# Cross-attention of a two-block transformer on one core: key/value chunks of 384 keys, projection units issued in halves and in alternation, the last batch's values projected last

## The chip, the cores and the metric

The kernel runs on one core of a Trainium2 chip. The metric is device time in microseconds (us) of one execution; the time before is the median of three runs.

## What is computed

The reference sends x (8 sequences of 64 tokens, 512 features) through a small cross-attention, self-attention, an FP4-rounded feed-forward layer, a second cross-attention, an RWKV time mix, a channel mix and a small KAN layer. The change touches the second cross-attention alone: 16 heads of 32 features, 64 queries per batch against the 1601 context tokens of that batch, with learned relative-position terms.

```python
q = query @ Wq + bq; k = key @ Wk + bk; v = value @ Wv + bv     # key = value = ctx (8, 1601, 512)
attn1 = einsum('bhqd,bhkd->bhqk', rq, rk)
attn2 = einsum('bhqd,qkd->bhqk', rq, rel_k_table[rel_idx])
attn = softmax((attn1 + attn2) / sqrt(32))
x = attn @ rv + einsum('bhqk,qkd->bhqd', attn, rel_v_table[rel_idx])
return x @ Wo + bo
```

## The kernel before

`cross_attention` is written engine by engine; each engine runs its own instruction stream in program order and meets the others at semaphores. The order of the work is one hand-made list per **period** (`period`, L858), and every engine walks the same list and picks its own part of each item. Period p projects keys and values of batch p and, beside that, turns and weighs batch p-1, so there are nine periods for eight batches; the ninth only attends.

**Chunks.** The context comes in six chunks per batch, one of 321 keys (`FIRST_CH`) and five of 256 (`CH`, L812). SyncE loads a chunk into one of two `ctx_raw` buffers (`load_ctx`, L968) as soon as the chunk before last has been split. GpSimd splits it (L1058, L1061) into a rounded part `ctx_hi` and a rest `ctx_lo`, each with two buffers of its own, once TensorE has projected the chunk before last.

**Items.** `u` is a projection unit of twelve matmuls (`unit`, L1073): a key unit makes 128 features by the keys of a chunk (moving width 322 or 256), a value unit makes 128 keys by 512 features. Within a chunk come four key units, then two or three value units. Units write PSUM banks 4 and 5 in turn, so a unit waits for the copy of the unit two before it; ScalarE copies keys (VectorE those of the first chunk), VectorE copies values. `s` is a score job (`scores`, L1118): queries by the keys of a chunk into banks 0 to 3, for eight heads of the first chunk or all sixteen of another, copied to `E` with a running maximum by VectorE (L1349). After the last of the seven jobs VectorE makes `peak` and ScalarE runs `exponentials` (L1245), eight instructions over all 1601 keys. `t` is a turn (`turn`, L1138): four transposes of `E` into bank 6, copied by ScalarE to `ET` (L1243); the next turn waits for that copy. `p` (`weigh`, L1161) multiplies `ET` by the values. `r` (`inverse`, L1179) spreads the inverse sums with sixteen matmuls from `diag`, which VectorE makes in `diagonals` (L1356); ScalarE copies the result to `spread` (L1257) and `normalise` (L1364) ends the batch.

**Order.** From the eighth unit of a period on there is a turn ahead of each unit and a weighing ahead of every second; `r` stands ahead of the last unit (index 35), the last score job behind it:

```python
            if j == T_GROUPS:
                out.append(("r", 0))
        out.append(("u", i))
        if i in S_AFTER:
            out.append(("s", S_AFTER[i]))
```

so ScalarE's stream has the copy to `spread` ahead of the exponentials of the next batch. SyncE's stream holds the chunk loads, the relative terms `corr` (`load_corr`, L978, two buffers), `exchange_near` (L988) and, at the end, the weights of the next layers, `w3o` first (L1034), which `cross_output` (L1404) needs.

Of the kernel before, what the change touches and what calls it, by code (L numbers as in the profile page):

```python
# [811 lines left out]
CH = 256  # L812
KT_TILES = -(-SK // P)
FIRST = SK - (KT_TILES - 1) * P
FIRST_CH = FIRST + 2 * P
FIRST_EVEN = FIRST_CH + FIRST_CH % 2
NCH = 1 + (SK - FIRST_CH) // CH
OCT = 2
PAIRS = 4 * OCT
V_RING, K_RING, ET_RING = KT_TILES + 3, 3, 4  # L820
T_GROUPS = 2 * KT_TILES + 2
P_GROUPS = KT_TILES + 1
K_UNITS, V_UNITS = KC * NCH, KT_TILES
# [12 lines left out]
def tiles_of_chunk(c):  # L836

    return range(0, 3) if c == 0 else range(2 * c + 1, 2 * c + 3)


UNITS = [u for c in range(NCH) for u in [("k", c, g) for g in range(KC)] + [("v", c, kt) for kt in tiles_of_chunk(c)]]
UNITS_FIRST = [("v", 0, kt) for kt in tiles_of_chunk(0)] + [("k", 0, g) for g in range(KC)] + UNITS[KC + 3:]
NU = len(UNITS)
S_JOBS = [(0, (0,)), (0, (1,))] + [(c, (0, 1)) for c in range(1, NCH)]
S_AFTER = {13: 0, 14: 1, 17: 2, 21: 3, 25: 4, 30: 5, 35: 6}
T_FROM = 7
DIAG_AFTER = 8


def s_outs(job):  # L850

    return sum(4 * len(octs) for _, octs in S_JOBS[:job])


S_OUTS = s_outs(len(S_JOBS))


def period(projects, attends):  # L858

    if not projects:  # L860
        out = [("t", 0), ("t", 1), ("diag", 0), ("t", 2)]
        for kt in range(P_GROUPS):
            out += [("p", kt)] + [("t", j) for j in (2 * kt + 3, 2 * kt + 4) if j < T_GROUPS]
        return out + [("r", 0), ("norm", 0)]
    out = []
    for i in range(NU):
        j = i - T_FROM
        if attends:
            if j >= 2 and j % 2 == 0 and j // 2 <= P_GROUPS:
                out.append(("p", j // 2 - 1))  # L870
            if 0 <= j < T_GROUPS:
                out.append(("t", j))
            if j == T_GROUPS:
                out.append(("r", 0))
        out.append(("u", i))
        if i in S_AFTER:
            out.append(("s", S_AFTER[i]))
        if attends and i == DIAG_AFTER:
            out.append(("diag", 0))
    return out + ([("norm", 0)] if attends else [])  # L880


def cross_attention(nc, sem, s, nm):
# [16 lines left out]
    ctx_lo = [m.tensor(f"ctx_lo{r}", [P, KC, (FIRST_EVEN, CH)[r]], F32R) for r in range(2)]  # L900
    K = [m.tensor(f"K{r}", [P, KC, FIRST_EVEN]) for r in range(K_RING)]
# [3 lines left out]
    corr = [m.tensor(f"corr{r}", [P, PAIRS, EDGE]) for r in range(2)]  # L905
# [5 lines left out]
    diag = m.tensor("diag", [P, PAIRS, P])  # L911
    relk, relv = m.tensor("relk", [P, SKEW]), m.tensor("relv", [EDGE, 2 * DH])
    kbias = m.tensor("kbias", [P, KC])
    one, ones = m.tensor("one", [P, 1]), m.tensor("ones", [P, DH])
# [15 lines left out]
    names = ("l_small zeroed p_zeroed one_set ones_set q_ps q_out v_hi v_lo k_hi k_lo dve_step bias_ready relk_ready "  # L930
             "split_hi split_lo k_ps v_ps k_out_act k_out_dve v_out rel_ps rel_out_act rel_out_dve "
             "s_ps corrected s_out peaked exped t_ps et_out pv_done r_ps r_out diag_done normed e_stored near_loaded").split()
    S = {n: sem("x_" + n) for n in names}
    ctx_loaded = [sem(f"x_ctx_loaded{r}") for r in range(2)]
    corr_loaded = [sem(f"x_corr_loaded{r}") for r in range(2)]
# [4 lines left out]

    units = lambda b: UNITS_FIRST if b == 0 else UNITS
    PERIODS = [(b, b - 1, period(b < B, b >= 1)) for b in range(B + 1)]
    on_dve = lambda unit: unit[0] == "k" and unit[1] == 0

    def k_done(b, unit):

        return b * K_UNITS + unit[1] * KC + unit[2] + 1

    def v_done(b, unit):

        return b * V_UNITS + unit[2] + 1

    def wait_copied(eng, b, unit):

        kind, c, j = unit
        if kind == "v":
            eng.wait_ge(S["v_out"], v_done(b, unit))
        elif on_dve(unit):
            eng.wait_ge(S["k_out_dve"], b * KC + j + 1)
        else:  # L960
            eng.wait_ge(S["k_out_act"], b * (K_UNITS - KC) + (c - 1) * KC + j + 1)

    def wait_scored(eng, q):

        b, c = divmod(q, NCH)
        eng.wait_ge(S["s_ps"], b * len(S_JOBS) + c + 2)

    def load_ctx(sp, q):  # L968

        b, c = divmod(q, NCH)  # L970
        r = q % 2
        if q >= 2:
            sp.wait_ge(S["split_lo"], q - 1)
        src = s.dram["ctx_first"][b] if c == 0 else s.dram["ctx"][b, c - 1]
        n = FIRST_EVEN if c == 0 else CH
        sp.dma_start(ctx_raw[r][:, :, 0:n], src).then_inc(ctx_loaded[r], 16)

    def load_corr(sp, b):  # L978

        if b >= 2:  # L980
            sp.wait_ge(S["corrected"], 2 * (b - 1))
        sp.wait_ge(rel_stored[b % 2], 16 * (b // 2 + 1))
        for p in range(PAIRS):
            at = rel_scr[b, p]
            skewed = bass.AP(at.tensor, at.offset + SQ - 1, [[SQ * SKEW, 2], [SKEW - 1, SQ], [1, EDGE]])
            sp.dma_start(corr[b % 2][:, p, :], skewed).then_inc(corr_loaded[b % 2], 16)
# [17 lines left out]
    with nc.Block() as block:  # L1004
        @block.sync
        def _(sp):
            load_ctx(sp, 0)
            sp.dma_start(bq[:], s.dram["b3q"]).then_inc(S["l_small"], 16)
# [5 lines left out]
            load_ctx(sp, 1)  # L1014
# [3 lines left out]
            load_ctx(sp, 2)  # L1018
# [7 lines left out]
            for bp, ba, items in PERIODS:  # L1026
                if bp == B:
                    exchange_near(sp, ba)
                    sp.wait_ge(S["k_ps"], B * K_UNITS)
                    sp.wait_ge(S["v_ps"], B * V_UNITS)  # L1030
                    sp.wait_ge(S["s_ps"], B * len(S_JOBS))
                    for n in ("w3o", "b3o", "vecs", "awk", "awv", "awr", "awo", "fwr"):
                        src = s.dram[n].partition_broadcast(P) if n == "b3o" else s.dram[n]
                        sp.dma_start(s.late[n][:], src).then_inc(s.loaded[n], 16)  # L1034
                    continue
                for c in range(NCH):
                    q = bp * NCH + c + 2
                    if 3 <= q < B * NCH:
                        load_ctx(sp, q)
                    if c == 1 and ba >= 0:  # L1040
                        exchange_near(sp, ba)
                    if c == 3 and bp + 1 < B:
                        load_corr(sp, bp + 1)

        @block.gpsimd
        def _(pool):
            nc.gpsimd.memset(one[:], 1.0).then_inc(S["one_set"], 1)
            nc.gpsimd.memset(zeros[:], 0.0).then_inc(S["zeroed"], 1)
            nc.gpsimd.memset(ones[:], 1.0).then_inc(S["ones_set"], 1)
            pool.wait_ge(S["one_set"], 1)  # L1050
            for q in range(B * NCH):
                r, n = q % 2, (FIRST_EVEN, CH)[q % NCH > 0]
                if q >= 2:
                    b, c = divmod(q - 2, NCH)
                    pool.wait_ge(S["k_ps"], b * K_UNITS + (c + 1) * KC)
                    pool.wait_ge(S["v_ps"], b * V_UNITS + tiles_of_chunk(c)[-1] + 1)
# [8 lines left out]
        def _(pe):  # L1065
# [7 lines left out]
            def unit(b, i):  # L1073
                kind, c, j = units(b)[i]
                q, n = b * NCH + c, b * NU + i
                r, dst = q % 2, bank(4 + n % 2)
                pe.wait_ge(S["split_lo"], q + 1)
                if n >= 2:
                    wait_copied(pe, *((b, units(b)[i - 2]) if i >= 2 else (b - 1, units(b - 1)[i - 2])))
                elif n < 2:  # L1080
                    pe.wait_ge(S["q_out"], KC)
                k = 0
# [903 lines left out]
```

## Time and profile before

| | |
|---|---|
| median of three runs | 1698.22 us (1698.11 to 1698.51) |
| the profiled execution's own time, its span | 1694.82 us, 1692.8 us |
| TensorE busy | 1464.5 us, 87% of the span |
| VectorE, ScalarE, GpSimd busy | 817.9, 488.9, 539.7 us (48%, 29%, 32%) |
| mean granted TensorE clock | 0.916 of 2.4 GHz |

The times are of one execution, taken by the profiler. PE is TensorE's matmuls, DVE is VectorE, ACT is ScalarE, POOL is GpSimd, SPq is SyncE's queue. "us" after a start is how long a group of like instructions took together; in brackets stands how long the engine was idle ahead of it and what ended the wait. A matmul's duration is longer than the distance to the next one, because matmuls are pipelined: costs of TensorE are read as the distance from one start to the next.

### The profile page before, as it was taken

The page shows a single profiled execution, that of the slowest core. Times are in us where ns is not written, and L with a number is a line of the kernel's source. Part 1 is how long each engine was busy: PE and PEld are TensorE (multiplying, and loading weights), DVE is VectorE, ACT ScalarE, POOL GpSimd, SP SyncE. Part 2 cuts the span into 40 slices and gives each one's busy share as a digit, 9 for nine tenths or more (in the row PEclk, how much of TensorE's full clock was granted, in tenths as well). Part 3 has the DMA queues.
Part 4 walks back from the last instruction along what each step waited for, and adds up shares of the span by engine and source line. Part 5 has one row for each costly group of instructions (what it writes and reads, how often), then busy time and mean ns, then how long its engine had stood idle before and what let it go on. Part 6 is the DMA issues. An engine that isn't in the chain of part 4 may idle for free. (4 is left out here: it accounts for less than half of the span.)

```text
span 1692.8 us, 29730 instructions
## 1 busy us (share of the span) xinstructions
PE 1464.5 (87%) x12488; PEld 1094.1 (65%) x12488; DVE 817.9 (48%) x1649; ACT 488.9 (29%) x832; POOL 539.7 (32%) x340
## 2 busy tenths in 40 slices
PE   8788977477988999999999999999999966936796
PEld 3556755244544788888888888888888843415573
DVE  2455289989434343243333333323333215978913
ACT  0323201041112115252342523434243351303302
POOL 6101057657322232232322222232322104616701
PEclk9788965688999999999999999999999988967997
DMA  5300020010102412111021111102111024003000
GB/s 233 149 1 1 25 112 1 0 69 0 75 0 80 152 47 62 35 40 57 26 64 32 44 52 39 54 30 57 39 43 40 2 85 191 0 0 119 0 0 25
DMA packets 54514, 88.19 MB, mean 52 GB/s; under 512 B 28784, under 2 KB 45424, under 8 KB 51312
## 3 DMA queue, kind: packets, MB, share of 16 engines
q1 hardware_dynamic: 54384, 86.31, 14.9%
q8 instruction: 100, 1.64, 0.4%
q14 instruction: 30, 0.25, 0.0%
HBM read 76.60 MB, written 9.70 MB: 51 GB/s over the span
## 5 line engine op out<-in xcount | busy, mean ns | idle before, releaser
L1058 POOL TENSOR_TENSOR ctx_hi<-ctx_raw,one 128x1024 fp32r<-128x1024 f32 (+1 forms) x48 | 94.5, 1970 | 590.6 <-issue 546.9
L1315 DVE TENSOR_TENSOR V<-PS,vbias 128x512 f32<-128x512 f32 (+1 forms) x104 | 71.8, 691 | 366.0 <-PE PS L1098 365.8
L1243 ACT COPY ET<-PS 128x512 f32<-128x512 f32 (+1 forms) x224 | 130.4, 587 | 287.5 <-PE PS L1158 287.4
L1349 DVE TENSOR_SCALAR_CACHE_REDUCE E<-PS 128x256 f32<-128x256 f32 (+1 forms) x384 | 141.1, 433 | 90.7 <-PE PS L1134 90.2
L1088 PE MATMUL PS<-ctx_hi,wk_hi 128*128 128x256 f32 (+1 forms) x768 | 139.9, 304 | 6.7 <-issue 6.7
L1158 PE MATMUL PS<-ident,E 128*128 128x128 f32 (+1 forms) x832 | 132.1, 284 | 13.2 <-ACT E L1250 12.5
L1088 PE MATMUL PS<-ctx_lo,wk_hi 128*128 128x256 f32 (+1 forms) x768 | 126.8, 287 | 0.0
L1088 PE MATMUL PS<-ctx_hi,wk_lo 128*128 128x256 f32 (+1 forms) x768 | 125.4, 285 | 0.0
L1225 ACT ACTIVATE K<-PS,kbias 128x256 f32<-128x256 f32 x160 | 76.1, 475 | 170.4 <-PE PS L1088 170.4
L1250 ACT ACTIVATE E<-E,peak 128x1601 f32<-128x1601 f32 x64 | 103.4, 1621 | 66.2 <-DVE peak L1354 66.2
L1061 POOL TENSOR_TENSOR ctx_lo<-ctx_raw,ctx_hi 128x1024 fp32r<-128x1024 f32 (+1 forms) x48 | 119.8, 2496 | 3.8
L1098 PE MATMUL PS<-wv_hi,ctx_hi 128*128 128x512 f32 (+1 forms) x416 | 120.2, 410 | 0.8 <-issue 0.8
L1158 PEld LDWEIGHTS PS<-ident,E 128*128 128x128 f32 (+1 forms) x832 | 93.3, 142 | 38.5 <-issue 25.9
L1088 PEld LDWEIGHTS PS<-ctx_hi,wk_hi 128*128 128x128 f32 x768 | 107.1, 190 | 13.3 <-issue 12.4
L1098 PE MATMUL PS<-wv_lo,ctx_hi 128*128 128x512 f32 (+1 forms) x416 | 113.6, 395 | 0.0
L1098 PE MATMUL PS<-wv_hi,ctx_lo 128*128 128x512 f32 (+1 forms) x416 | 113.5, 394 | 0.0
L1088 PEld LDWEIGHTS PS<-ctx_lo,wk_hi 128*128 128x128 f32 x768 | 108.3, 190 | 0.0
L1088 PEld LDWEIGHTS PS<-ctx_hi,wk_lo 128*128 128x128 f32 x768 | 107.1, 189 | 0.0
L1098 PEld LDWEIGHTS PS<-wv_lo,ctx_hi 128*128 128x128 f32 (+1 forms) x416 | 76.5, 184 | 20.3
L1098 PEld LDWEIGHTS PS<-wv_hi,ctx_lo 128*128 128x128 f32 (+1 forms) x416 | 76.4, 184 | 20.1
L1098 PEld LDWEIGHTS PS<-wv_hi,ctx_hi 128*128 128x128 f32 (+1 forms) x416 | 70.5, 185 | 18.9 <-issue 6.9
L1174 PE MATMUL PS<-ET,V 128*32 128x64 f32 (+1 forms) x3328 | 68.4, 223 | 2.4 <-ACT ET L1243 2.4
(282 smaller groups left out, 2415.2 us busy)
## 6 DMA issues: line engine op xcount, KB each, us to landing
ctx_raw<-in_ctx SPq DMA_DIRECT2D x40, 512.0 KB, 3.7
ctx_raw<-in_ctx_first SPq DMA_DIRECT2D x8, 644.0 KB, 3.9
rel_scr<-rel_out SPq DMA_DIRECT2D x8, 640.0 KB, 4.0
fwk<-in_fwk SPq DMA_DIRECT2D x1, 4096.0 KB, 12.4
fwv<-in_fwv SPq DMA_DIRECT2D x1, 4096.0 KB, 12.8
corr<-rel_scr SPq DMA_DIRECT2D x64, 48.0 KB
p_scr<-E SPq DMA_DIRECT2D x16, 192.0 KB, 2.1
near<-p_scr SPq DMA_DIRECT2D x64, 48.0 KB
```

What stands on the lines that cost most here:

```text
L1058: nc.gpsimd.tensor_tensor(ctx_hi[r][:, :, 0:n], ctx_raw[r][:, :, 0:n], one[:].unsqueeze(1).broadcast_to([P, KC, n]), ALU.mult).then_inc(S[ ...
L1061: nc.gpsimd.tensor_tensor(ctx_lo[r][:, :, 0:n], ctx_raw[r][:, :, 0:n], ctx_hi[r][:, :, 0:n].bitcast(F32), ALU.subtract).then_inc(S["split_ ...
L1088: last = nc.tensor.matmul(dst[:, 0:cols], w[:, kc, j * P:(j + 1) * P], x[:, kc, 0:cols], start=(k == 0), stop=(k == 3 * KC - 1))
L1098: last = nc.tensor.matmul(dst[0:rows, :], x[:, kc, k0:k0 + rows], w[:, kc, :], start=(k == 0), stop=(k == 3 * KC - 1))
L1158: last = nc.tensor.transpose(dst[0:n, r * P:(r + 1) * P], src(4 * o + r), s.ident[:])
L1174: last = nc.tensor.matmul(bank(BANK_O)[32 * r:32 * r + 32, g * SQ:(g + 1) * SQ], value, ET[0:n, (2 * kt + o) % ET_RING, r * P + gg * SQ:r ...
L1225: nc.scalar.activation(K[q % K_RING][:, j, 0:n], bank(4 + (b * NU + i) % 2)[:, 0:n], ACT.Identity, bias=kbias[:, j:j + 1]).then_inc(S["k_o ...
L1243: nc.scalar.copy(ET[0:n, j % ET_RING, :], src[0:n, :]).then_inc(S["et_out"], 1)
L1250: nc.scalar.activation(E[:, p, :], E[:, p, :], ACT.Exp, scale=scale, bias=peak[:, p:p + 1], accum_out=total[:, p:p + 1]).then_inc(S["exped ...
L1315: v.tensor_tensor(V[0:rows, at % V_RING, :], bank(4 + (b * NU + i) % 2)[0:rows, :], vbias[0:rows, :], ALU.add).then_inc(S["v_out"], 1)
L1349: v.tensor_scalar(E[:, p, k0:k0 + n], bank(r)[:, at:at + n], 1.0, None, ALU.mult, ALU.max, accum_out=tops[:, p, c:c + 1]).then_inc(S["s_ou ...
```

## The change

Chunks become one of 449 keys and three of 384. `units_of_visit` alternates key and value units in all chunks but the first of all and a batch's last one; in that last one the value units stay behind the keys. A unit is issued as two halves of six matmuls, and a period is laid out on half-unit slots. In the last batch all four chunks are visited for keys (period 7) and then loaded and split again for values (period 8). `ctx_lo` lies in the memory of `ctx_raw`, so a load waits until the chunk before last is fully projected. Score jobs are eight, of eight heads each. The inverse sums go through one 128x8 transpose, a ScalarE copy of eight rows, and two matmuls with a selection matrix `sel`; both steps of `r` close the period. `corr` has one buffer.

```diff
-CH = 256
+CH = 384
-V_RING, K_RING, ET_RING = KT_TILES + 3, 3, 4
+V_RING, ET_RING = KT_TILES + TPC + 1, 4
+S_JOBS = [(c, o) for c in range(NCH) for o in range(OCT)]
+VISITS = [(b, c, "kv") for b in range(B - 1) for c in range(NCH)] + [(B - 1, c, kind) for kind in "kv" for c in range(NCH)]
+def units_of_visit(q):
+    b, c, kinds = VISITS[q]
+    ks = [("k", q, b, c, g) for g in range(KC)] if "k" in kinds else []
+    vs = [("v", q, b, c, kt) for kt in tiles_of_chunk(c)] if "v" in kinds else []
+    if kinds == "kv" and 0 < q and c < NCH - 1:
+        return [u for pair in zip(ks, vs) for u in pair] + ks[len(vs):] + vs[len(ks):]
+    return vs + ks if q == 0 else ks + vs
+def period(p):
+    slots = 2 * len(UNITS[p])
+    at = [[] for _ in range(slots + 8)]
+    put = lambda slot, item: at[min(slot, slots + 7)].append(item)
+    if p == B - 1:
+        turns, lag, scored = (lambda j: 16 + j // 2), 1, (21, 22, 24, 25, 27, 28, slots, slots)
+    elif p == B:
+        turns, lag, scored = (lambda j: 12 + j // 2), 1, ()
+    else:
+        turns, lag, scored = (lambda j: 13 + 44 * j // T_GROUPS), 2, (26, 28, 36, 38, 46, 48, 54, 56)
+    if p >= 1:
         for kt in range(P_GROUPS):
+            put(max(turns(2 * kt + 1) + lag, 2 * kt + 4 if p == B else 0), ("p", kt))
+        for j in range(T_GROUPS):
+            put(turns(j), ("t", j))
+    for job, slot in enumerate(scored):
+        put(slot, ("s", job))
     out = []
+    for slot in range(slots + 8):
+        out += sorted(at[slot], key=lambda item: "pts".index(item[0]))
+        if slot < slots:
+            out.append(("u", slot))
+    if p >= 1:
+        out += [("r", 0), ("r", 1), ("norm", 0)]
+    return out
...
-    ctx_lo = [m.tensor(f"ctx_lo{r}", [P, KC, (FIRST_EVEN, CH)[r]], F32R) for r in range(2)]
+    ctx_lo = [m.rounded(f"ctx_raw{r}") for r in range(2)]
...
         if q >= 2:
-            sp.wait_ge(S["split_lo"], q - 1)
+            wait_projected(sp, q - 2)
...
-                dst = bank((BANK_T, 4, 5)[j % 3] if last_batch else BANK_T)
+                dst = bank((BANK_T, 0, 1)[j % 3] if last_batch else BANK_T)
...
+            def spread_inverse(b, step):
+                if step == 0:
+                    pe.wait_ge(S["et_out"], T_GROUPS * (b + 1))
+                    pe.wait_ge(S["inverted"], b + 1)
+                    last = nc.tensor.transpose(bank(BANK_T)[0:PAIRS, 0:P], inverse[:], s.ident[:])
+                else:
+                    pe.wait_ge(S["r_out"], 2 * b + 1)
+                    pe.wait_ge(S["l_small"], 16 * 7)
+                    for o in range(OCT):
+                        last = nc.tensor.matmul(bank(BANK_T)[:, o * P:(o + 1) * P], sel[:, o, :], inverse_rows[:], start=True, stop=True)
                 last.then_inc(S["r_ps"], 1)
...
+            def inverse_copy(b, step):
+                act.wait_ge(S["r_ps"], 2 * b + step + 1)
+                if step == 0:
+                    nc.scalar.copy(inverse_rows[:], bank(BANK_T)[0:PAIRS, 0:P]).then_inc(S["r_out"], 1)
+                else:
+                    if b >= 1:
+                        act.wait_ge(S["normed"], b)
+                    nc.scalar.copy(spread[:], bank(BANK_T)[:, 0:OCT * P]).then_inc(S["r_out"], 1)
+            for p, ba, items in PERIODS:
                 for kind, k in items:
...
                     elif kind == "s" and k == len(S_JOBS) - 1:
-                        exponentials(bp)
+                        exponentials(p)
                     elif kind == "r":
-                        inverse_copy(ba)
+                        inverse_copy(ba, k)
```

In periods 1 to 6 the list built from this ends: `s6 u54 t27 u55 s7 u56 p13 u57 r0 r1 norm`, where u54 to u57 are the halves of the last two value units. Period 7 ends: `u29 p13 u30 u31 s6 s7 r0 r1 norm`, with key halves.

## Rows read from the trace of the kernel before

**Rows 1.** Busy time by engine over one full period: PE, PEld, DVE, ACT, POOL, clock

```profile
736.70:840.90 104.20, 102.65 (x1214) 86.57 (x1213) 37.07 (x128) 39.05 (x65) 26.76 (x12) 1.00 0.15 45
```

**Rows 2.** Timeline, start us and us: the first matmuls of periods 2 and 7

```profile
736.79 0.76 PE L1088 MATMUL PS<-ctx_hi,wk_hi 128*128 128x322 f32 x4
...
1257.71 0.76 PE L1088 MATMUL PS<-ctx_hi,wk_hi 128*128 128x322 f32 x4
```

**Rows 3.** Timeline of the end of period 7, TensorE, VectorE and ScalarE

```profile
1355.09 0.37 ACT L1257 COPY spread<-PS 128x256 f32<-128x256 f32 x1 [0.57 <-PE PS L1185]
...
1357.95 1.12 PE L1134 MATMUL PS<-K,qT 32*64 32x256 f32 x32
...
1359.18 0.43 DVE L1349 TENSOR_SCALAR_CACHE_REDUCE E<-PS 128x256 f32<-128x256 f32 x1 [0.43 <-PE PS L1134]
...
1361.59 0.42 DVE L1349 TENSOR_SCALAR_CACHE_REDUCE E<-PS 128x256 f32<-128x256 f32 x1
...
1362.50 1.63 ACT L1250 ACTIVATE E<-E,peak 128x1601 f32<-128x1601 f32 x1 [7.04 <-DVE peak L1354]
...
1375.32 0.19 ACT L1250 ACTIVATION_READ_ACCUMULATOR E<-E,peak 128x1 f32 x1
```

**Rows 4.** Timeline of TensorE: a turn, a weighing, a turn, a key unit, a turn

```profile
707.23 0.65 PE L1174 MATMUL PS<-ET,V 128*32 128x64 f32 x32
707.82 0.66 PE L1158 MATMUL PS<-ident,E 128*128 128x128 f32 x4
708.23 0.72 PE L1088 MATMUL PS<-ctx_hi,wk_hi 128*128 128x256 f32 x4
...
709.74 0.60 PE L1158 MATMUL PS<-ident,E 128*128 128x128 f32 x4
```

**Rows 5.** Timeline of TensorE: TensorE restarts after a wait in period 0

```profile
581.87 1.38 PE L1134 MATMUL PS<-K,qT 32*64 32x321 f32 x16 [4.05 <-DVE E L1349]
583.18 1.22 PE L1088 MATMUL PS<-ctx_hi,wk_hi 128*128 128x256 f32 x4
...
585.53 0.64 PE L1088 MATMUL PS<-ctx_hi,wk_hi 128*128 128x256 f32 x4
```

**Rows 6.** Windows as in rows 1, after the wait for the last exponentials

```profile
1377.00:1381.00 4.00, 4.00 (x75) 3.10 (x73) 0.44 (x3) 2.00 (x4) 0.00 (x0) 0.58 0.10 22
```

**Rows 7.** Timeline of TensorE: uninterrupted units of width 322 and 512

```profile
743.35 0.76 PE L1088 MATMUL PS<-ctx_hi,wk_hi 128*128 128x322 f32 x4
...
745.14 1.08 PE L1098 MATMUL PS<-wv_hi,ctx_hi 128*65 128x512 f32 x4
...
747.91 1.09 PE L1098 MATMUL PS<-wv_hi,ctx_hi 128*128 128x512 f32 x4
```

**Rows 8.** Timeline of TensorE: the two waits of a period

```profile
739.71 0.84 PE L1088 MATMUL PS<-ctx_hi,wk_hi 128*128 128x322 f32 x4 [0.96 <-issue]
...
771.53 0.80 PE L1134 MATMUL PS<-K,qT 32*64 32x321 f32 x16
...
774.92 0.80 PE L1134 MATMUL PS<-K,qT 32*64 32x321 f32 x16 [0.59 <-DVE E L1349]
```

**Rows 9.** Timeline of SyncE's queue in period 0

```profile
565.52 9.55 SPq L986 DMA_DIRECT2D corr<-rel_scr  x8
```

**Rows 10.** The two split instructions: duration ns min/median/max, starts, forms

```profile
L1058 POOL TENSOR_TENSOR ctx_hi<-ctx_raw,one x48: 1894/1897/2338, 525.9 to 1326.9; 128x1024 fp32r<-128x1024 f32 x40, 128x1288 fp32r<-128x1288 f32 x8
L1061 POOL TENSOR_TENSOR ctx_lo<-ctx_raw,ctx_hi x48: 2360/2390/2969, 528.3 to 1328.9; 128x1024 fp32r<-128x1024 f32 x40, 128x1288 fp32r<-128x1288 f32 x8
```

**Rows 11.** DMA issues: KB each, median us from issue to landing

```profile
ctx_raw<-in_ctx SPq DMA_DIRECT2D x40, 512.0 KB, 3.7
...
w3o<-in_w3o SPq DMA_DIRECT2D x1, 1024.0 KB, 6.5
```

**Rows 12.** Costliest groups: busy us, mean ns of one, idle before and releaser

```profile
L1243 ACT COPY ET<-PS 128x512 f32<-128x512 f32 (+1 forms) x224 | 130.4, 587 | 287.5 <-PE PS L1158 287.4
```

**Rows 13.** Timeline: VectorE's last instruction of the stage

```profile
1405.85 0.42 DVE L1367 TENSOR_TENSOR YT<-PS,spread 128x256 f32<-128x256 f32 x1 [28.41 <-ACT spread L1257]
```

More of the change, by code:

```diff
@@ L836, in tiles_of_chunk @@
 def tiles_of_chunk(c):
[L838 to L852, printed above, removed]
@@ L855 @@
[L855 to L861, printed above, removed]
-        for kt in range(P_GROUPS):
-            out += [("p", kt)] + [("t", j) for j in (2 * kt + 3, 2 * kt + 4) if j < T_GROUPS]
-        return out + [("r", 0), ("norm", 0)]
-    out = []
[L866 to L880, printed above, removed]
+    return range(0, TPC + 1) if c == 0 else range(TPC * c + 1, TPC * (c + 1) + 1)
@@ new lines, with on_dve, counted @@
+ORDER = [u for units in UNITS for u in units]
+NUMBER = {u: n for n, u in enumerate(ORDER)}
+def on_dve(unit):
+    kind, q, b, c, j = unit
+    return kind == "k" and (c == 0 or (b == B - 1 and c == 1))
+def counted(of):
+    return {u: n + 1 for n, u in enumerate(u for u in ORDER if of(u))}
+K_NTH, V_NTH = counted(lambda u: u[0] == "k"), counted(lambda u: u[0] == "v")
+K_DVE_NTH, K_ACT_NTH = counted(on_dve), counted(lambda u: u[0] == "k" and not on_dve(u))
+LAST_OF_VISIT = [units_of_visit(q) for q in range(len(VISITS))]
@@ L883, in cross_attention @@
+PERIODS = [(p, p - 1, period(p)) for p in range(B + 1)]
 def cross_attention(nc, sem, s, nm):
@@ L904, in cross_attention @@
     ET = m.tensor("ET", [P, ET_RING, D])
-    corr = [m.tensor(f"corr{r}", [P, PAIRS, EDGE]) for r in range(2)]
+    corr = m.tensor("corr", [P, PAIRS, EDGE])
     near = m.tensor("near", [P, PAIRS, EDGE])
@@ L1094, in unit @@
                     k0 -= keys_of_chunk(c)[0]
[L1095 to L1101 removed]
+                    products = [(dst[0:rows, :], x[:, kc, k0:k0 + rows], w[:, kc, :])
+                                for w, x in ((wv_hi, ctx_hi[r]), (wv_lo, ctx_hi[r]), (wv_hi, ctx_lo[r])) for kc in range(KC)]
+                half = len(products) // 2
+                for k in range(half * second, half * (second + 1)):
+                    last = nc.tensor.matmul(*products[k], start=(k == 0), stop=(k == 2 * half - 1))
+                if second:
+                    last.then_inc(S[kind + "_ps"], 1)
             def relative(b):
@@ L1314, in v_copy @@
                     dve.wait_ge(S["pv_done"], ob * P_GROUPS + okt + 1)
[L1315 removed]
+                v.tensor_tensor(V[0:rows, at % V_RING, :], bank(4 + NUMBER[unit] % 2)[0:rows, :], vbias[0:rows, :],
                                 ALU.add).then_inc(S["v_out"], 1)
```

309 lines of the change are left out of this document (136 added, 173 removed).

## The prediction

> **What bounds the kernel now.** I read the busy time by window first. In a full period of the cross-attention TensorE is busy 102.65 of 104.20 us at the full granted clock of 2.4 GHz [rows 1]; no other engine reaches 40. Periods follow each other every 104.18 us: (1257.71 - 736.79) / 5 [rows 2]. So nothing but TensorE's own work and its waits counts here. Of waits a period has two of any size, 0.96 us near its start and 0.59 us at the second score job [rows 8]. The timeline at a period's end shows why there are no more. ScalarE copies `spread` at 1355.09, then the score job, its eight copies and the maximum run, and the exponentials go from 1362.50 to 1375.51, 13.0 us in which ScalarE serves nobody else [rows 3]. TensorE does not need ScalarE then: the next seven units are copied by VectorE, and the first turn comes behind them.
>
> **The wait that the change adds.** Both steps of `r` now close the list, behind the last score job. ScalarE walks the same list, so the copy of eight rows that step 0 needs stands behind `exponentials`. TensorE's step 1 waits for that copy, and all units of the next period are queued behind step 1. I count both sides from the start of job s7.
>
> ScalarE: the job of 32 matmuls has its first copy 1.23 us after its start; with 16 matmuls of width 384 the job is between 0.80 us (16 of width 321 [rows 8]) and 1.12 us, so I take 1.0 us. Copies come every (1361.59 - 1359.18) / 7 = 0.344 us; at 384 wide that is between 0.344 and 0.52, I take 0.48, nearer to proportion. The last of four starts at 2.4. From there to the first exponential it is 0.91 us [rows 3], with the longer copy 1.05: 3.5. The exponentials add 13.0, the small copy about 0.4 with its handover (the `spread` copy of twice the width took 0.37): TensorE goes on at 16.9.
>
> TensorE: s7 costs about 0.85; each value half is six matmuls at 0.231 (a value unit is 747.91 - 745.14 = 2.77 us [rows 7]), 1.39 and 0.09 to restart after another kind of work; the weighing 0.59 (707.82 - 707.23 [rows 4]) and 0.09; the small transpose 0.1. Together 4.6. **TensorE stands for 16.9 - 4.6 = 12.3 us** in each of periods 1 to 6. Bounds from the choices above: 11.6 to 12.9. Period 0 has no `r`.
>
> Restart: after a wait of 4.05 us the score job took 1.38 instead of 0.80 us and the key unit 585.53 - 583.18 = 2.35 instead of 1.51 us (709.74 - 708.23), together 1.4 us lost to the lower granted level of 1.2 GHz [rows 4, 5]. After the longer wait for the last exponentials the mean granted clock was still 0.58 in the four microseconds from 1377, where TensorE was fully busy [rows 6], so 3.4 of them ran at half rate. For a 12 us wait I take 2.0 us lost, between 1.4 and 3.4.
>
> **The rest of a period.** Width: a matmul of width 322 comes every 1.79 / 12 = 0.149 us, one of 512 every 0.231 [rows 7]. On the line between them 384 costs 0.176 and 450 costs 0.204; 256 costs (1.51 - 0.09) / 12 = 0.118. Keys of a batch: 4 x 1.79 + 20 x 1.42 = 35.6 before; 4 x 12 x 0.204 + 12 x 12 x 0.176 = 35.1 after. The columns are the same 1602 per group, only the fixed part goes: -0.5. Score jobs: before 5 x 1.05 and 2 x 0.73, as busy times less the overlap of 0.07; after six at about 0.84 and two at about 0.94: +0.2. Seven weighings no longer share their place with a turn, and there is a job more: about eight restarts of 0.09 and smaller turns (0.35 alone, 0.41 behind a weighing), +0.5 at most. Both old waits go, -0.96 and -0.59: the first because VectorE has drained during the new wait, the second because s0 and s1 are a whole value unit and a turn apart, 3.9 us and more, against the 3.39 us of today [rows 8] plus 0.5 for longer copies. Sum -1.4. The larger split (1.5 x 1.90 and 1.5 x 2.39 [rows 10]) plus loading (3.7 for 512 KB [rows 11], I take 4.2 for 768) is 11.0 us from one chunk's last unit to the next but one's first; it has the visit between, 4 x 2.1 + 3 x 2.77 = 16.7 us and its turns, as cover. Each of periods 1 to 6: -1.4 + 12.3 + 2.0 = +12.9, **six of them +77.4 us**.
>
> **Period 0.** The third chunk is now loaded behind the `corr` issues, which take 9.55 us [rows 9]. The eight relative jobs end later by four us because the first visit is longer, so the load is issued near 579 and the chunk is split near 592, while units and score jobs of the second visit carry TensorE to about 588. With s1 waiting for `corr` as s1 does now, waits are about 6 to 7 us instead of 4.05 [rows 5]: +2.6.
>
> **The last batch.** Today it takes 1406.27 - 1257.71 = 148.6 us from its first matmul to the last normalisation [rows 2, 13], with 13 us of exponentials bare. After, period 7: first two key visits 9.9 + 8.4; the third chunk is ready 11.0 us after the first visit ends, against 8.4 of cover, wait 2.6; then fourteen slots with two turns on one bank, where the second waits for the first's copy: 0.66 + 0.59 + 0.05 = 1.3 us [rows 4, 12] instead of 0.41, then 0.41, a key half 1.15, a weighing 0.68, so 3.55 x 14 = 49.7; six score jobs 5.2; two last halves 2.1; key copy and s6 with its copies 3.9; and again 16.9 to the end of the exponentials and the row copy, because s7, r0 and r1 stand side by side ahead of all value units. Sum 98.7. Period 8: values 36.0, slow restart 2.0, chunk wait 1.0, turns 14 x 0.86 = 12.0, weighings 14 x 0.65 = 9.1, r0, copy, r1, copy, normalise 2.4, and `w3o`, now issued only when the last value unit is done, lands 6.5 us later [rows 11], about 2.2 us after TensorE wants it. Sum 64.7. Together 163.4: **+14.8 us**. The value units held back to cover the exponentials cover nothing, since TensorE reaches them only behind r1.
>
> Sum: 77.4 + 2.6 + 14.8 = +94.8 on the profiled execution's 1694.8 us, 1789.6; the median of the runs is 3.4 us above it, so **1793 us**.
>
> **A rule against my width term.** The steps of 0.118, 0.149 and 0.231 us rise nearly with the columns, and that is what the sum uses. The Trainium skill, TensorE: Matmul & The Clock Gate, Back-to-back issue gap, gives for a sustained stream of load and matmul pairs 81 ns at 128 columns and 131 ns at 512. By a line through its two figures keys would gain some 6 us a batch instead of 0.5.
>
> **Rivals.**
> *TensorE is not held* (other side): the row copy gets to ScalarE ahead of the exponentials, or TensorE has enough other work there. Place: between s7 and r1. For it: today's `spread` copy does stand ahead of them. Against: the new list. It decides where TensorE's own work behind s7 reaches 15.5 us instead of 4.6. Then periods 1 to 6 give -1.4 each, period 0 +2.6, the last batch 163.4 - 13.0 - 2.0 = 148.4, no change: 1692 us. 4%.
> *Chunk supply becomes the bound*: load, both splits and projection now follow each other through one buffer pair. It decides if the 11.0 us were above 16.7. For it: `ctx_lo` now overwrites `ctx_raw`, whose in-place price no row shows; against: the separate-buffer rows would have to grow by half. One us on each of 30 visits adds 30: 1823 us. 5%.
> *Wide matmuls are much cheaper per column*: for it nothing here, since 322 and 512 lie on one line with 256; eight batches times 5.5 us less gives 1749 us. The page named above says so. 1%.
>
> **How the numbers follow.** Forecast 89%, the rivals 10%, something else 1%. The range takes the wait's bounds (7 x 0.7 both ways), the restart's (7 x -0.6, 7 x +1.4), the paired turns of period 7, which are worth 12 us if they overlap after all, and half of the supply rival's way: 1770 to 1815. A measurement of this kernel can tell about 0.2% from no change. Faster 4%, within 1%, slower 95%.
>
> **What would show it.** Right: in six periods an idle stretch of about 12 us on TensorE ahead of two matmuls that read `sel` and `inverse_rows`, ended by ScalarE's copy to `inverse_rows`, right behind eight exponentials; one of about 16 us ahead of the first value unit of the last batch; periods of about 117 us; clock at 1.2 GHz at each restart; key matmuls of width 384 every 0.176 us. Wrong: periods near 103 us, the row copy ahead of the exponentials, or TensorE waiting for splits.

## The result, and the profile after

| | before | after |
|---|---|---|
| median | 1698.37 us (four runs) | 1793.12 us (1789.96 to 1796.12, four runs) |
| the profiled execution's own time, its span | 1694.82, 1692.8 us | 1796.12, 1794.3 us |
| TensorE busy, mean granted clock | 1464.5 us, 0.916 | 1486.7 us, 0.893 |

The changed kernel takes 1.0557 times as long (95% interval 1.0534 to 1.058). It is slower, and by about the amount forecast.

Per period of the profiled executions, from the first key matmul to that of the next (the same form as [rows 2]; period 0 from its first value matmul, at 539.68 before and 542.27 after):

| stretch | before, us | after, us | difference | predicted |
|---|---|---|---|---|
| period 0 | 92.9 | 93.1 | +0.2 | +2.6 |
| periods 1 to 6 together | 625.1 | 702.8 (115.35, then 116.8 to 118.2 each) | +77.7 | +77.4 |
| last batch to its normalisation | 148.6 | 168.4 | +19.8 | +14.8 |
| ahead of period 0, and after the stage | | | +2.6, +1.2 | none |

The profile page's busy times and its group of the two-step `r` and of TensorE's wait ahead of it (busy us, mean ns of one, then the idle time before and its releaser):

```profile
PE 1486.7 (83%) x11120; PEld 1074.5 (60%) x11120; DVE 776.5 (43%) x1333; ACT 465.4 (26%) x772; POOL 557.5 (31%) x315
...
L1201 PE MATMUL PS<-inverse_rows,sel 8*128 8x128 f32 x32 | 9.2, 436 | 89.8 <-ACT inverse_rows L1269 89.8
```

The 89.8 us are six waits of 11.90, one of 18.03 in period 7 and one of 0.34 in the last period, where no score job precedes `r`. The timeline of the end of period 1, which answers to [rows 3], shows one of the six:

```profile
732.91 0.90 PE L1147 MATMUL PS<-K,qT 32*64 32x384 f32 x16
...
733.92 0.56 DVE L1359 TENSOR_SCALAR_CACHE_REDUCE E<-PS 128x384 f32<-128x384 f32 x1 [0.21 <-PE PS L1147]
...
735.36 0.55 DVE L1359 TENSOR_SCALAR_CACHE_REDUCE E<-PS 128x384 f32<-128x384 f32 x1
...
736.38 1.64 ACT L1263 ACTIVATE E<-E,peak 128x1601 f32<-128x1601 f32 x1 [4.19 <-DVE peak L1364]
...
737.41 0.27 PE L1196 MATMUL PS<-ident,inverse 128*8 128x128 f32 x1
...
749.20 0.19 ACT L1263 ACTIVATION_READ_ACCUMULATOR E<-E,peak 128x1 f32 x1
749.30 0.24 ACT L1269 COPY inverse_rows<-PS 8x128 f32<-8x128 f32 x1
...
749.59 1.22 PE L1201 MATMUL PS<-inverse_rows,sel 8*128 8x128 f32 x4 [11.90 <-ACT inverse_rows L1269]
...
750.73 1.87 PE L1114 MATMUL PS<-ctx_hi,wk_hi 128*128 128x450 f32 x4
...
755.18 1.10 PE L1114 MATMUL PS<-wv_hi,ctx_hi 128*65 128x512 f32 x4
```

Read it from the bottom. TensorE could have gone on at 737.7. What it waits for is a copy of eight rows that takes 0.24 us, and that copy stands behind 12.9 us of exponentials of the next batch, because ScalarE works through its list in order. The key unit behind it then runs at half speed: its first four matmuls take 1.87 us of busy time against 0.98 for four of the same width in an uninterrupted stretch (the last fence of the part on why the prediction was right). The windows over period 2 and over the four microseconds behind the wait (the columns are those of [rows 1]):

```profile
750.73:868.11 117.38, 105.48 (x1043) 84.55 (x1042) 30.29 (x87) 36.35 (x58) 25.88 (x8) 0.94 0.13 39
749.59:753.59 4.00, 4.00 (x12) 3.47 (x13) 0.42 (x1) 0.37 (x1) 0.00 (x0) 0.50 0.20 49
```

A granted clock of 0.50 is the 1.2 GHz level; a full period now has TensorE idle for 117.38 - 105.48 = 11.90 us, all of it this one wait, against 1.55 in [rows 1].

TensorE's timeline at the end of period 7, where the wait is longest:

```profile
1416.98 0.86 PE L1114 MATMUL PS<-ctx_hi,wk_lo 128*128 128x384 f32 x4
1418.71 0.91 PE L1147 MATMUL PS<-K,qT 32*64 32x384 f32 x16 [0.88 <-ACT K L1238]
1421.77 1.59 PE L1147 MATMUL PS<-K,qT 32*64 32x384 f32 x16 [2.15 <-DVE E L1359]
1423.29 0.38 PE L1196 MATMUL PS<-ident,inverse 128*8 128x128 f32 x1
1441.69 1.21 PE L1201 MATMUL PS<-inverse_rows,sel 8*128 8x128 f32 x4 [18.03 <-ACT inverse_rows L1269]
1442.84 1.97 PE L1114 MATMUL PS<-wv_hi,ctx_hi 128*65 128x512 f32 x4
```

The value units that were held back to fill this stretch begin at 1442.84, when the exponentials are over.

### The profile page after: what moved, and what is told of

Same layout as the page of the kernel before. It is cut to its first block and busy times, and to the rows that moved or that the text cites. A ratio compares the mean times of both kernels' runs of the same rounds, so it can differ in the third digit from the quotient of the medians.

```text
span 1794.3 us, 26535 instructions
## 1 busy us (share of the span) xinstructions
PE 1486.7 (83%) x11120; PEld 1074.5 (60%) x11120; DVE 776.5 (43%) x1333; ACT 465.4 (26%) x772; POOL 557.5 (31%) x315
## 5 line engine op out<-in xcount | busy, mean ns | idle before, releaser
L1074 POOL TENSOR_TENSOR ctx_hi<-ctx_raw,one 128x1536 fp32r<-128x1536 f32 (+1 forms) x36 | 102.9, 2858 | 725.6 <-DMA ctx_raw<-in_ctx 560.9
L1359 DVE TENSOR_SCALAR_CACHE_REDUCE E<-PS 128x384 f32<-128x384 f32 (+1 forms) x256 | 131.8, 571 | 124.4 <-PE PS L1147 123.8
L1114 PE MATMUL PS<-ctx_raw_r,wk_hi 128*128 128x384 f32 (+1 forms) x512 | 135.8, 367 | 0.0
L1077 POOL TENSOR_TENSOR ctx_raw_r<-ctx_raw,ctx_hi 128x1536 fp32r<-128x1536 f32 (+1 forms) x36 | 130.6, 3628 | 2.8
L1114 PE MATMUL PS<-ctx_hi,wk_hi 128*128 128x384 f32 (+1 forms) x512 | 128.0, 373 | 3.1 <-POOL ctx_raw_r L1077 3.1
L1114 PE MATMUL PS<-ctx_hi,wk_lo 128*128 128x384 f32 (+1 forms) x512 | 117.0, 351 | 0.0
L1114 PE MATMUL PS<-wv_hi,ctx_raw_r 128*128 128x512 f32 (+1 forms) x416 | 114.2, 396 | 0.0
L1114 PEld LDWEIGHTS PS<-ctx_raw_r,wk_hi 128*128 128x128 f32 x512 | 93.4, 197 | 5.6 <-issue 1.9
L1238 ACT ACTIVATE K<-PS,kbias 128x384 f32<-128x384 f32 x92 | 53.5, 581 | 137.4 <-PE PS L1114 137.4
L1114 PEld LDWEIGHTS PS<-wv_hi,ctx_raw_r 128*128 128x128 f32 (+1 forms) x416 | 76.8, 185 | 20.6 <-issue 0.8
L1201 PE MATMUL PS<-inverse_rows,sel 8*128 8x128 f32 x32 | 9.2, 436 | 89.8 <-ACT inverse_rows L1269 89.8
```

Source lines behind the costliest of these rows:

```text
L1074: nc.gpsimd.tensor_tensor(ctx_hi[r][:, :, 0:n], ctx_raw[r][:, :, 0:n], one[:].unsqueeze(1).broadcast_to([P, KC, n]), ALU.mult).then_inc(S[ ...
L1077: nc.gpsimd.tensor_tensor(ctx_lo[r][:, :, 0:n], ctx_raw[r][:, :, 0:n], ctx_hi[r][:, :, 0:n].bitcast(F32), ALU.subtract).then_inc(S["split_ ...
L1114: last = nc.tensor.matmul(*products[k], start=(k == 0), stop=(k == 2 * half - 1))
L1201: last = nc.tensor.matmul(bank(BANK_T)[:, o * P:(o + 1) * P], sel[:, o, :], inverse_rows[:], start=True, stop=True)
L1238: nc.scalar.activation(K[c][:, j, 0:n], bank(4 + NUMBER[unit] % 2)[:, 0:n], ACT.Identity, bias=kbias[:, j:j + 1]).then_inc(S["k_out_act"], 1)
L1359: v.tensor_scalar(E[:, p, k0:k0 + n], bank(r)[:, 0:n], 1.0, None, ALU.mult, ALU.max, accum_out=tops[:, p, c:c + 1]).then_inc(S["s_out"], 1)
```

## The experiments

The theory: nothing but the place of `r` makes the time; the wait and the restart behind it are the whole of the loss, and alternation, chunk size, single buffers and the held-back values are worth little. The rivals were the alternation (supply of chunks, copies in another order) and the last batch's new layout.

**1. r ahead of the last score job, in all periods or in period 7 alone.** One place in the list is changed; what is computed is the same.

```diff
     if p >= 1:
-        out += [("r", 0), ("r", 1), ("norm", 0)]
+        at_r = out.index(("s", len(S_JOBS) - 1)) if p < B else len(out)
+        out[at_r:at_r] = [("r", 0), ("r", 1)]
+        out.append(("norm", 0))
```

For period 7 alone the condition is `p == B - 1`.

> The changed kernel with both steps of r placed ahead of the last score job in the list of every period that has one; norm stays last. Theory (ScalarE serves its list in order, so the eight-row copy waits only for what stands ahead of it): in periods 1 to 6 the 11.9 us wait turns into a round trip of about 0.6 us, and the 2 us restart at half clock goes; ahead of the last batch's values the 18.0 us wait and its restart go. 6 x (11.3 + 2.0) + 20 = 100 us less than the changed kernel's 1793: 1693 us, periods of 104 us. Rival (the wait only moves: something else, the first turn behind the exponentials, the supply of chunks or VectorE, needs the same time): at least half of each wait comes back elsewhere, 1740 us or more. Rival (it is not the order but the larger chunks): within 10 us of 1793.

> The same move of r, in period 7 alone. Theory: only the wait of 18.0 us ahead of the held-back value units and its slow restart go, since six value units (17 us) then cover the exponentials: 1793 - 20 = 1773 us. Rival (the value units held back do not cover them, the first turn waits instead): 1783 us or more.

Measured: 1688.9 us (1687.48 to 1691.05), ratio 0.9936 [0.992, 0.9953] to the kernel before; and 1772.38 us, 1.0433 [1.0417, 1.0448]. The timeline of the first, at the place where the changed kernel stood for 11.90 us:

```profile
733.27 0.26 ACT L1271 COPY inverse_rows<-PS 8x128 f32<-8x128 f32 x1 [0.93 <-PE PS L1198]
...
733.58 0.71 PE L1203 MATMUL PS<-inverse_rows,sel 8*128 8x128 f32 x4 [0.34 <-ACT inverse_rows L1271]
...
734.22 0.90 PE L1149 MATMUL PS<-K,qT 32*64 32x384 f32 x16
...
737.69 1.64 ACT L1265 ACTIVATE E<-E,peak 128x1601 f32<-128x1601 f32 x1 [2.99 <-DVE peak L1366]
```

The round trip through ScalarE costs TensorE 0.34 us when ScalarE is free. Periods fall to 103.19 us, the last batch to 147.0. With only period 7 corrected the same group keeps six of the waits, 6 x 11.90 + 2 x 0.34 = 72.1:

```profile
L1203 PE MATMUL PS<-inverse_rows,sel 8*128 8x128 f32 x32 | 8.7, 416 | 72.1 <-ACT inverse_rows L1271 72.1
```

So the place of `r` costs 1793.1 - 1688.9 = 104.2 us, of which 20.7 in period 7 and 83.5 in the six others, 13.9 each. What is left of the change is a gain of 0.6%, where 1692 was given for the rival in which TensorE is not held and 1693 in the expectation, 3 and 4 us too much. No run takes back the chunk size or the half units alone, so how the 0.6% divides between them is not shown.

**2. The other direction: the kernel before with its one-step r behind the last score job.** No other part of the change is made.

```diff
                 out.append(("t", j))
-            if j == T_GROUPS:
-                out.append(("r", 0))
         out.append(("u", i))
...
-    return out + ([("norm", 0)] if attends else [])
+    return out + ([("r", 0), ("norm", 0)] if attends else [])
```

> The kernel before with its one-step r moved behind the last score job, where the change has its two steps. TensorE itself waits for nothing of ScalarE there. Theory (a copy queued behind the exponentials holds whoever waits for it, and whoever waits for them): norm on VectorE waits for the copy to spread, VectorE's key copies of the next period stand behind norm, and TensorE stops at the third unit of the next period, about 10.9 us, plus 2 us restart, less the 0.96 us wait of today: +11.9 us in six periods and 1 us at the end, 1698 + 73 = 1771 us. Rival (only a TensorE that waits for ScalarE directly loses the time; the one-step form is safe anywhere): 1698 us within 3.

Measured: 1778.03 us (1774.52 to 1782.26), 1.0465 [1.0446, 1.0484]. The place alone costs the old kernel some 79 us. The way to TensorE is a longer one here:

```profile
741.24 0.64 PE L1183 MATMUL PS<-diag,ones 128*32 128x128 f32 x16
...
741.45 1.90 POOL L1056 TENSOR_TENSOR ctx_hi<-ctx_raw,one 128x1024 fp32r<-128x1024 f32 x1 [12.16 <-issue]
741.55 1.82 DVE L1352 TENSOR_SCALAR peak<-peak 128x8 f32<-128x8 f32 x1
...
743.40 1.64 ACT L1248 ACTIVATE E<-E,peak 128x1601 f32<-128x1601 f32 x1 [9.18 <-DVE peak L1352]
...
756.32 0.35 ACT L1255 COPY spread<-PS 128x256 f32<-128x256 f32 x1
...
756.70 0.42 DVE L1365 TENSOR_TENSOR YT<-PS,spread 128x256 f32<-128x256 f32 x1 [12.73 <-ACT spread L1255]
757.04 1.00 DVE L1302 TENSOR_SCALAR K<-PS,kbias 128x321 f32<-128x321 f32 x2
...
757.68 1.41 PE L1086 MATMUL PS<-ctx_hi,wk_hi 128*128 128x322 f32 x4 [11.60 <-issue]
```

TensorE issues `r` and two key units, then wants a bank. VectorE, which must copy those units out, stands at the normalisation, which waits for `spread`, which ScalarE copies behind the exponentials. One in-order queue holds the next. My figure was 7 us low. The six waits are 11.60 us each and not 10.9, which makes 4.2 of it. I had also priced the scaling of the peaks, the VectorE row at 741.55, at 0.17 us, its cost in period 7 of the old kernel, and it takes 1.82 in the others (experiment 5); the rest was not followed.

**3. The alternation and the held-back values.** First the alternation undone in the changed kernel, then in the kernel of experiment 1; then the kernel of experiment 1 with the last batch projected like any other (visits `range(B)` with keys and values, the last period turns and weighs only). The second diff shows the main line; the list of the last two periods, the loads and the engine of one chunk's key copies follow from it.

```diff
-    if kinds == "kv" and 0 < q and c < NCH - 1:
-        return [u for pair in zip(ks, vs) for u in pair] + ks[len(vs):] + vs[len(ks):]
     return vs + ks if q == 0 else ks + vs
```

```diff
-VISITS = [(b, c, "kv") for b in range(B - 1) for c in range(NCH)] + [(B - 1, c, kind) for kind in "kv" for c in range(NCH)]
+VISITS = [(b, c, "kv") for b in range(B) for c in range(NCH)]
```

> The changed kernel with all keys of a chunk ahead of its values again, the alternation alone undone. Theory (in steady periods TensorE is busy either way, and the order within a chunk decides no wait): within 3 us of the changed kernel, 1790 to 1796 us. Rival (alternation spaces the copies of ScalarE and VectorE and removes waits of units for their bank): 1.0 us or more in each of 8 periods, 1801 us or more. The other sign, keys first being quicker: 1785 or less.

> As the run with r ahead in all periods (1688.9 us), with all keys of a chunk ahead of its values. Theory (alternation decides no wait): 1688.9 within 2 us. Rival (without the long waits, in which VectorE and ScalarE catch up, the order within a chunk starts to matter): 4 us or more to either side.

> As the run with r ahead in all periods (1688.9 us), and the last batch projected like all others (keys and values in one visit, the ninth period only attends, as in the kernel before); chunks, halves and alternation as changed. Theory (held-back values cover the exponentials, but the same period pays for it with fourteen pairs of turns on one bank, 0.95 instead of 0.4 us for the second, with slower restarts and a second load and split): the two cancel, since that run's last batch takes 147.1 us and the kernel before's 148.6; 103.2 + 43.5 = 146.7 us expected here, so 1688 to 1691 us. Rival (holding back gains what it covers, 13 us): 1700 us or more.

Measured: 1792.44 us (1790.39 to 1796.12) with keys first against 1793.12 with alternation; 1689.87 against 1688.9 in the kernel with `r` first; 1688.81 (1688.05 to 1693.69) without the held-back values. None of the three can be told from its partner. The alternation shows no effect in either kernel. The values held back cover nothing in the changed kernel. In the one with `r` first they do cover the exponentials, since their last batch shows no wait for them, while the normally projected one waits twice:

```profile
1361.87 1.09 PE L1173 MATMUL PS<-ident,E 128*65 128x128 f32 x4 [5.50 <-ACT E L1266]
1368.31 1.94 PE L1173 MATMUL PS<-ident,E 128*65 128x128 f32 x8 [5.36 <-ACT E L1266]
```

Still both last batches take 147 us (1254.67 to 1401.69 with, 1253.02 to 1399.88 without). The cover saves two waits of 10.9 us together. In the kernel with `r` first, period 7 has fourteen waits of 0.68 us, 9.5 together, where two turns follow each other on one bank. That these take back what the cover gives is a sum of rows; experiment 4 takes away half of them.

**4. Making more of the layout.** Turns of period 7 spread over its slots instead of two in each; then also the third chunk loaded ahead of the first `corr`.

```diff
     if p == B - 1:
-        turns, lag, scored = (lambda j: 16 + j // 2), 1, (21, 22, 24, 25, 27, 28, slots, slots)
+        turns, lag, scored = (lambda j: 11 + 3 * j // 4), 1, (21, 22, 24, 25, 27, 28, slots, slots)
```

```diff
+            load_ctx(sp, 2)
             load_corr(sp, 0)
...
-                    if 2 <= q:
+                    if 3 <= q:
```

> As the run with r ahead in all periods (1688.9 us), with the turns of period 7 spread from two in each of 14 slots (16 + j // 2) to slots 11 to 31 (11 + 3j // 4). Theory (the second of two turns on one bank waits 0.68 us for ScalarE's copy): seven pairs instead of fourteen, 7 x 0.55 = 3.9 us, and the 0.88 us wait for the third chunk is filled with turns: 1684 to 1685 us. Rival (the first turns now wait for the exponentials of the period before, which end about 16.5 us after the last score job): no gain, 1689.

> As the run before it (turns spread), and SyncE issues the load of the third chunk ahead of the eight corr loads. Theory: the 2.1 us wait for the split in period 0 goes, the 1.8 us wait for corr stays or grows by the time of the load, and less is lost at half clock: 1 to 3 us less than the run with the turns spread, about 1682 us. Rival (corr then lands later by as much): the same as that run.

Measured: 1685.55 us (1684.14 to 1687.07), 0.9918 [0.9906, 0.9931], and 1682.98 us (1682.28 to 1684.3), 0.9904 [0.9891, 0.9918]. The turns in pairs had shown waits of 0.67 us, fourteen times; in the changed kernel:

```profile
1362.96 0.66 PE L1170 MATMUL PS<-ident,E 128*128 128x128 f32 x4
1364.29 0.66 PE L1170 MATMUL PS<-ident,E 128*128 128x128 f32 x4 [0.68 <-ACT ET L1256]
```

Spread, the last batch takes 141.6 instead of 147.0 us, with seven such waits left; the wait for the third chunk, which the turns were to fill, stays at 0.94. The two profiled executions lie 5.5 us apart, the medians 3.4: the profiled one of experiment 1 was the longest of its four. The earlier load replaces two waits of 2.16 and 2.12 us in period 0 by one of 3.83 (below, in the second kernel), since `corr` now comes later. That is 0.45 us. The profiled executions lie 1.4 us apart, of which 1.0 stands ahead of the stage, and the intervals of the two ratios overlap, so the 2.6 us between the medians are no measure of the earlier load.

```profile
587.94 1.29 PE L1150 MATMUL PS<-K,qT 32*64 32x449 f32 x16 [3.83 <-DVE E L1362]
```

**5. The instruction of 128x8 elements that takes up to 2.75 us.** In the changed kernel the scaling of the peaks takes 0.17 us in seven periods and 2.75 in period 7; before, it was 1.82 in seven and 0.17 in one. The last wait of TensorE is longer by it. In the kernel before, the 0.96 us wait of [rows 8] stands behind it too. The end of that chain in period 2:

```profile
737.09 1.90 POOL L1058 TENSOR_TENSOR ctx_hi<-ctx_raw,one 128x1024 fp32r<-128x1024 f32 x1 [12.61 <-issue]
737.20 1.82 DVE L1354 TENSOR_SCALAR peak<-peak 128x8 f32<-128x8 f32 x1
...
738.93 0.68 DVE L1315 TENSOR_TENSOR V<-PS,vbias 128x512 f32<-128x512 f32 x1
```

The copy at 738.93 empties a bank, and the unit that had waited starts at 739.71, 0.1 us after it. The two rows of period 7 of the changed kernel:

```profile
1425.01 3.42 POOL L1077 TENSOR_TENSOR ctx_raw_r<-ctx_raw,ctx_hi 128x1536 fp32r<-128x1536 f32 x1
...
1425.71 2.75 DVE L1364 TENSOR_SCALAR peak<-peak 128x8 f32<-128x8 f32 x1
```

Both end at 1428.4. To find what form of instruction is held, the product with a number became a product with a constant column, in the changed kernel and in the kernel before:

```diff
-                    v.tensor_scalar(peak[:], peak[:], -scale, None, ALU.mult).then_inc(S["peaked"], 1)
+                    v.tensor_tensor(peak[:], peak[:], minus[:].broadcast_to([P, PAIRS]), ALU.mult).then_inc(S["peaked"], 1)
```

> The changed kernel, with the scaling of the 128x8 peaks written as a product of two tensors (against a constant column) instead of a product with a number. In the changed kernel this small VectorE instruction takes 0.17 us where GpSimd stands idle and up to 2.75 us where a chunk's split runs on GpSimd, and the exponentials of its query block start behind it. Theory: the one-operand form is what waits for GpSimd's split; then the product form takes under 0.3 us in all eight instances, the exponentials of the last query block start 2.5 us earlier, the last wait of TensorE for the copy of r is 15.5 instead of 18.0 us, and the kernel takes 1790.5. Rival: any small VectorE instruction waits for the split that runs; then the longest instance stays at 1.5 to 3 us and the time at 1793.

> The kernel before, with the scaling of the peaks as a product of two tensors instead of a product with a number. In the kernel before seven of its eight instances start 0.11 us after GpSimd's first split instruction of 1.90 us and take 1.82 us, ending with it; the eighth has no split beside it and takes 0.17. The exponentials are not waited for in those seven periods, so the time should stay at 1698 to 1700 whatever the instruction takes; the row decides. Theory A, only the one-operand form waits for GpSimd: 0.17 us in all eight. Theory B, a product of two tensors that lie in SBUF waits as well: 1.8 us in seven again. B is what the Trainium skill, SBUF, has in its part on the shared port pair (a VectorE instruction in a mode of two ports, or with two inputs in SBUF, blocks until GpSimd's running instruction has ended). If GpSimd's split starts after the product instead, its own duration grows and neither is decided.

In the changed kernel (1792.79 us, one run, where the first theory gave 1790.5 and the rival 1793) all eight took 0.17 us and the last wait was 15.56 us, both as the first theory had it. But the rows show that the question had not been put: in that run the product started 0.09 us ahead of the second split.

```profile
1425.28 0.17 DVE L1367 TENSOR_TENSOR peak<-peak,minus 128x8 f32<-128x8 f32 x1
1425.37 3.44 POOL L1078 TENSOR_TENSOR ctx_raw_r<-ctx_raw,ctx_hi 128x1536 fp32r<-128x1536 f32 x1
```

What put it there was s7, which took 0.91 us in this run and 1.59 in the changed kernel, and not the form: where s7 took 0.91 with `r` first in period 7 alone, the product with a number took 0.17 too.

```profile
1424.35 0.17 DVE L1366 TENSOR_SCALAR peak<-peak 128x8 f32<-128x8 f32 x1
1424.35 3.56 POOL L1079 TENSOR_TENSOR ctx_raw_r<-ctx_raw,ctx_hi 128x1536 fp32r<-128x1536 f32 x1
```

The kernel before puts the question, in seven periods (1700.03 us beside 1700.05 for the kernel before in the same runs):

```profile
741.09 1.89 POOL L1059 TENSOR_TENSOR ctx_hi<-ctx_raw,one 128x1024 fp32r<-128x1024 f32 x1 [12.62 <-issue]
741.19 1.81 DVE L1357 TENSOR_TENSOR peak<-peak,minus 128x8 f32<-128x8 f32 x1
```

The product of two tensors waits just as long, in all seven instances that start 0.10 us after a split, and not in the eighth. My first theory falls: the one-operand form is not what matters. The Trainium skill, SBUF: State Buffer, Who interferes with whom, says that a VectorE instruction in a mode of two ports, or with two inputs in SBUF beside a GpSimd instruction that reads SBUF, blocks until the running GpSimd instruction has ended. These rows agree for the form with two inputs; the form with one is held just the same, but no row shows in which mode it ran. The score copies, which read PSUM and also write an accumulator, are not held: in period 0 of the changed kernel those of width 449 take 0.62 us beside a split (590.80) and 0.62 ahead of one (586.76).

Last, the scaling was taken out of the best kernel: the score copies multiply by the negative scale and keep the minimum, which is the bias itself.

```diff
-                    v.tensor_scalar(E[:, p, k0:k0 + n], bank(r)[:, 0:n], 1.0, None, ALU.mult, ALU.max,
+                    v.tensor_scalar(E[:, p, k0:k0 + n], bank(r)[:, 0:n], -scale, None, ALU.mult, ALU.min,
...
-                    ch.link(v.tensor_reduce(peak[:], tops[:], AX.X, ALU.max))
-                    v.tensor_scalar(peak[:], peak[:], -scale, None, ALU.mult).then_inc(S["peaked"], 1)
+                    v.tensor_reduce(peak[:], tops[:], AX.X, ALU.min).then_inc(S["peaked"], 1)
```

> The best kernel so far (r ahead of the last score job, turns of period 7 spread, third chunk loaded ahead of corr), and the separate scaling of the peaks taken out: the score copies multiply by the negative scale and keep the minimum, the reduction over the chunks is a minimum and is the bias itself, and the exponentials take scale -1. The same function up to rounding. The scaling instruction took up to 3.2 us beside GpSimd's split in period 7 of the kernel that this is made from, and the exponentials of the last batch start behind it; there they are waited for only if the work held back does not cover them. Theory: in that kernel 13 us of exponentials stand beside some 36 us of value units, so they are covered and the time stays at 1683; rival: they are on the path, the time falls by 3 to 1680.

Measured: 1682.17 us (1680.8 to 1683.65), 0.9896 [0.9879, 0.9914]. Against 1682.98 that is no difference, as the theory had it: once value units cover the exponentials, 3.2 us at their start cost next to nothing (the kernel with the scaling shows one wait of 0.27 us for the first exponential).

## Why the prediction was right

**The wait, predicted 12.3 us, measured 11.90, six times.** ScalarE's side was counted as 16.9 us from the start of s7, and is 749.59 - 732.91 = 16.68. TensorE's side was 4.6, and is 737.68 - 732.91 = 4.77. Both sizes held to 0.25 us, worked out from rows of the same or like instructions.

**The restart, predicted 2.0.** `r1` and the next key unit take 755.18 - 749.59 = 5.59 us against 0.64 and 12 x 0.204 at full clock, so 2.5 us are lost, 0.5 more than I took and within its bounds. The upper bound of 3.4 was misread, though: it is the time at half rate in [rows 6], of which half is lost, 1.7 us. The key unit's part of the loss, about 2 us, falls in the following period: period 1 takes 115.35 us and periods 2 to 6 117.5 on average.

**The rest of a period, predicted -1.4.** In the kernel with `r` first a period is 103.19 us with a round trip of 0.34 in it, so 102.85 without: -1.33 against the 104.18 of before. Both old waits are gone, as forecast, but the reason given for the first, that VectorE drains during the new wait, is not what counts: it is gone in the kernel with `r` first too, which has no long wait in these periods. There the scaling of the peaks takes 0.17 us and not the 1.82 behind which the old wait stood (experiment 5). No run takes the scaling out of the old kernel alone. The term for the widths held; TensorE's timeline in the first two key visits of period 7:

```profile
1347.37 0.98 PE L1114 MATMUL PS<-ctx_hi,wk_hi 128*128 128x450 f32 x4
1348.19 0.98 PE L1114 MATMUL PS<-ctx_raw_r,wk_hi 128*128 128x450 f32 x4
...
1350.54 0.86 PE L1114 MATMUL PS<-ctx_raw_r,wk_hi 128*128 128x384 f32 x4
1351.24 0.87 PE L1114 MATMUL PS<-ctx_hi,wk_lo 128*128 128x384 f32 x4
```

Four matmuls of width 384 come in 0.70 us, 0.175 each, where the line through the old rows gave 0.176; four of width 450 in 0.82, where it gave 4 x 0.204. The rival of much cheaper wide matmuls falls, since the measured spacing decides, and so does the chunk supply: beyond period 0 only one wait for a split is left, 0.97 us in period 7.

**Period 0, predicted +2.6, measured +0.2: over-sized.** The step "the chunk is split near 592, ... waits are about 6 to 7 us" had the waits too long. They are 1.89 us for the score copies and 2.15 for the split, 4.04 together, like the 4.05 of [rows 5].

**The last batch, predicted +14.8, measured +19.8: under-sized.** By stretches:
- To the start of s7: 83.6 us against 81.8. The first key visit takes 1349.83 - 1338.15 = 11.7 us instead of 9.9, since it follows a wait; I had put each restart into the period of its wait and so left this one out of period 7. The third chunk's wait is 0.97 instead of 2.6. The fourteen slots, their score jobs and the last halves take 58.5 us against 49.7 + 5.2 + 2.1 = 57.0. Most of the 1.5 is the score jobs: a slot without one takes 3.55 us, as forecast, one with a job 4.57 to 4.69, so six jobs cost 6.4 us and not 5.2. The key copy and s6 are 4.1 against 3.9.
- From s7 to the row copy's release of TensorE: 1441.69 - 1421.77 = 19.9 against "again 16.9". The step took the peaks at their length in the old period 7. They take 2.75 us, 2.6 more, beside GpSimd's split; and s7 itself ran at the lower clock after its own wait of 2.15 us, 1.59 us of busy time instead of 0.90.
- From there to the end: 64.9 against 64.7.

**The level.** Predicted 94.8 between medians, measured 94.75; between the two profiled executions it is 101.3, to which the table's rows add up within 0.2. Two of its parts lie outside the change's terms: the stage starts 2.6 us later, after a granted clock of 0.52 instead of 0.83 between 520 and 530 us, and 1.2 us follow the stage. The later start is no effect of the change: with the same code ahead, the kernels of experiments 1 and 4 start the stage between 539.8 and 542.6. So the agreement to a microsecond is partly luck: the profiled execution of after was the longest of its four, 3.0 us above the median, and that of before 3.6 below its own. The two misses also offset each other in part, 2.4 us too much in period 0 and 5.0 too little in the last batch. What held is the one large term. The upper end of the range, 1815, does not follow from its parts, which add up to 1823; the result does not depend on it.

## What to carry to other kernels

In a kernel whose engines each work through one list in order, a short hand-over costs what stands ahead of it on the engine that serves it. Before an item is moved in a shared list, ask of every engine what long job it is now behind, and who stands behind the engine that waits for it: here a copy of 0.24 us, one position too late in the list, cost 14 us in each of six periods and 21 in the seventh. Work kept back as cover helps only if it stands ahead of the wait in the queue of the engine that is to be kept busy.

## What the hardware showed that I had not expected

A VectorE instruction of 128x8 elements took 0.17 us alone and 1.82, 2.75 and, in the second kernel of experiment 4, 3.22 us when a GpSimd split had started before it; each time it ended within 0.04 us of the split's end. It holds for a product with a number and for a product of two tensors in SBUF alike. Placed ahead of a chain it must be timed by what GpSimd does at that moment, not by its size.

The score job s7 ran at about half speed (1.59 us of busy time instead of 0.90, granted clock 0.50) after a wait of 2.15 us in the changed kernel, and equally after one of 0.89 in the kernel with `r` first. In the kernel with the product form it took 0.91 after a wait of 2.15, and with `r` first in period 7 alone 0.91 after the same 0.89, both at a granted clock of 1.00:

```profile
1336.57 1.59 PE L1149 MATMUL PS<-K,qT 32*64 32x384 f32 x16 [0.89 <-DVE E L1361]
1421.09 0.91 PE L1149 MATMUL PS<-K,qT 32*64 32x384 f32 x16 [0.89 <-DVE E L1361]
```

The first row is of the kernel with `r` first in all periods, the second of the one with period 7 alone. Ahead of the first row the clock fell although no wait of TensorE in that period is longer than 0.89 us. These runs do not say what decides it. Two waits of the same length can so differ by 0.7 us behind them.
